# Message passing over 200,000 edges: nodes of layer 0 normalised once, 5 and 3 of 68 tiles fetched by column copies, edge features loaded three blocks at a time

## The reference

```python
edge_index = jnp.stack([src, dst])
h = relu(layernorm(x))
# layer 0
agg = segment_sum(h[src], dst)
x = x + agg @ W_rel.T + b_rel + h @ W_root.T
h = relu(layernorm(x))
# layer 1
edge_weights = silu(edge_attr_50 @ We1 + be1) @ We2 + be2
agg = segment_sum(h[src] * edge_weights, dst)
x = x + (h + silu(agg @ Wn1 + bn1) @ Wn2 + bn2)
```

## Time and profile before

| | |
|---|---|
| median of 3 runs | 5615.37 us (5615.32 to 5629.94) |
| span of the profiled execution, first to last instruction | 3996.3 us |
| that execution's own time with what lies around the span | not given by the profile |
| gathers | 2 x 1564, 67% of the chain that ended last |
| layer 0, first to last gather | 3.5 to 1964.1 us |
| layer 1, first to last gather | 2011.3 to 3976.7 us |
| busy: POOL, PE, DVE, ACT | 2976, 2447, 1995, 1187 us |

### The profile page before, as it was taken

How to read it: one execution, slowest core, us unless ns; L and a number is a source line. 1 busy time by engine, 2 the same in 40 slices (tenths; PEclk the granted TensorE clock), 3 DMA queues, 4 the chain that set the end, 5 groups by cost and what they waited for, 6 DMA issues and landing times.

```text
span 3996.3 us, 52113 instructions
## 1 busy us (share of the span) xinstructions
PE 2447.1 (61%) x10946; PEld 1882.0 (47%) x10946; DVE 1995.0 (50%) x6931; ACT 1187.2 (30%) x2730; POOL 2976.2 (74%) x3135
## 2 busy tenths in 40 slices
PE   3444444444444444444467788877887777887787
PEld 2334333333433333433445555555555555555555
DVE  6555555555555555555554444444444444444444
ACT  3444444444444444444411111111111111111111
POOL 7777777777777777777567777777777777777776
PEclk8555555555555555555578788788788887888878
DMA  2222222222222222222122222222222222222222
GB/s 84 62 61 61 61 64 67 61 61 61 61 64 67 61 61 61 61 66 64 50 78 78 83 80 79 81 76 83 78 80 82 77 75 83 80 79 82 77 76 82
DMA packets 208083, 284.73 MB, mean 71 GB/s; under 512 B 70338, under 2 KB 137972, under 8 KB 207828
## 3 DMA queue, kind: packets, MB, share of 16 engines
q0 software_dynamic: 100096, 205.20, 18.1%
q1 hardware_dynamic: 66676, 58.00, 4.9%
q10 hardware_dynamic: 41184, 20.45, 1.7%
HBM read 262.97 MB, written 20.45 MB: 71 GB/s over the span
## 4 chain that ended last, share of the span: by engine, by line
POOL 67%; issue 23%; PE 5%; DMA 2%; DVE 1%; POOLq 1%; ACT 0%; SPq 0%; DVEq 0%; ACTq 0%
POOL rows L298 67%; PE hid_ps L368 2%; PE seg_a L330 1%; PE ew_ps L373 1%; DMA rows<-h_rows,idx 1%; PE seg_b L330 1%; DMA ef<-ef_blocks 1%; POOLq L176 1%; POOLq L177 0%; DVE rows L670 0%; DVE onehot L566 0%; DVE ew_ps L666 0%; ACT hidden L502 0%; PE node_t L382 0%; ACT rows L436 0%
## 5 line engine op out<-in xcount | busy, mean ns | idle before, releaser
L298 POOL DMA_INDIRECT rows<-h_rows,idx x1564 | 1490.0, 953 | 522.6 <-issue 515.6
L298 POOL DMA_INDIRECT rows<-x,idx x1564 | 1485.2, 950 | 478.2 <-issue 478.2
L330 PE MATMUL seg_a<-onehot,rows 128*128 128x128 f32 x3312 | 726.6, 388 | 915.0 <-DVE onehot L566 408.1
L330 PEld LDWEIGHTS seg_a<-onehot,rows 128*128 128x128 f32 x3312 | 623.7, 281 | 1148.5 <-issue 960.0
L330 PE MATMUL seg_b<-onehot,rows 128*128 128x128 f32 x2944 | 606.4, 370 | 530.9 <-DVE onehot L566 374.4
L424 ACT ACTIVATE rows<-rows,e_shift,e_rstd 128x128 f32<-128x128 f32 x1564 | 643.3, 481 | 793.0 <-DVE e_shift L593 793.0
L330 PEld LDWEIGHTS seg_b<-onehot,rows 128*128 128x128 f32 x2944 | 520.8, 266 | 727.6 <-issue 448.3
L502 ACT ACTIVATE hidden<-hid_ps,be_col 128x512 f32<-128x512 f32 x391 | 268.8, 687 | 1416.1 <-PE hid_ps L368 1415.8
L373 PE MATMUL ew_ps<-we_sb,hidden 128*128 128x128 f32 x3128 | 539.8, 330 | 49.1 <-ACT hidden L502 49.1
L582 DVE BATCH_NORM_STATS2 e_stats<-rows 128x6 f32<-128x128 f32 x1564 | 339.7, 280 | 426.1 <-DMA rows<-x,idx 361.8
L368 PE MATMUL hid_ps<-ef,we_sb 50*128 50x512 f32 x782 | 522.7, 753 | 39.4 <-DMA ef<-ef_blocks 39.4
(11 more groups left out here) (91 smaller groups left out, 811.5 us busy)
## 6 DMA issues: line engine op xcount, KB each, us to landing
ef<-ef_blocks SPq DMA_DIRECT2D x391, 100.0 KB
rows<-x,idx POOLq DMA_INDIRECT x1564, 2.5
rows<-h_rows,idx POOLq DMA_INDIRECT x1564, 2.5
xs<-x SPq DMA_DIRECT2D x26, 256.0 KB
y_rows<-ys ACTq DMA_DIRECT2D x26, 256.0 KB, 2.5
ys<-y_rows SPq DMA_DIRECT2D x26, 256.0 KB, 3.3
out<-xs ACTq DMA_DIRECT2D x26, 256.0 KB
h_rows<-h1s ACTq DMA_DIRECT2D x24, 256.0 KB, 2.5
```

The costliest lines, as they stand in the source:

```text
L298: pool.indirect_dma_start(out=rows[:, u, t, :], out_offset=None, in_=table, in_offset=bass.IndirectOffsetOnAxis(ap=idx[:, j:j + 1], axis=0 ...
L330: mm = pe.matmul(seg[u % 2][:, 0:P], rows[:, u, t, :], onehot[:, u % 2, t, :], start=(t == 0), stop=(t == TB - 1))
```

## The change

Three parts.

- **Layer 0 is normalised per node.** A new phase ahead of layer 0 takes the 25 node groups of `x` through statistics, shift and ReLU once (five sets of buffers, `H_SETS`), stores them to a new table `h_rows` in HBM, turns them on PE and copies the turned groups into `agg[1]`, which is free during layer 0 (`h_table`: one column to a node). Iteration 0 of layer 0 works as before on rows of `x`; iterations 1 to 22 gather from `h_rows` and have no edge statistics and no ReLU. `node_update0` takes its turned group from `h_table`.
- **Some tiles are not gathered.** In iterations 1 to 22 of layer 0 the last 5 of the 68 tiles, in layer 1 the last 3, are made from the table in SBUF: an engine reads 16 node numbers from `cp_idx` into registers and copies 16 single columns (128 x 1) of the table into `act_cols` or `dve_cols`, eight times for a tile. ACT makes 3 tiles in layer 0 and 2 in layer 1, DVE 2 and 1. PE turns a finished tile into PSUM, and ACT copies it from there into `rows` (`rows_turned`). For layer 1 the table (`agg[0]`) is filled between the layers by 25 groups of turns of `h1_rows`.
- **Edge features** come in loads of three blocks into two buffers, in place of one block into four slots.

```diff
-EF_SLOTS = 4
+EF_BLOCKS = 3
+EF_GROUPS = -(-U // EF_BLOCKS)
+H_SETS = 5
+CHUNK = 16
+CHUNKS = P // CHUNK
+H_BY_ACT = (3, 4)
+CP_ACT = (3, 2)
+CP_DVE = (2, 1)
+CP_TILES = CP_ACT[0] + CP_DVE[0]
+CP_FIRST = U * TB - CP_TILES
...
+        cp_idx = sb("cp_idx", [ITERS, CP_TILES * P], I32)
+        act_cols, dve_cols = sb("act_cols", [P, 3 * P]), sb("dve_cols", [P, 2 * P])
...
+        ef = [sb("ef_a", [D_EDGE, EF_BLOCKS, BLOCK])[:, :, :], node_work[0:D_EDGE, :, :]]
...
+        h_table, h1_table = agg[1], agg[0]
...
+        def indices(engine, it, first, count):
+
+            row = bass.at_runtime_partition(cp_idx[0:1, first:first + count], it)
+            _, values = nc.values_load_multi_w_load_instructions(
+                row, engines=[engine], min_val=0, max_val=N_NODES - 1,
+                skip_runtime_bounds_check_because="edge sources are node numbers")
+            return values
...
@@ SP, ahead of layer 0
+            def load_h(k, r):
+                sp.dma_start(h_x[r], node_group(x, k * H_SETS + r)).then_inc(s_hx[r], 16)
+
+            def store_h(k, r):
+                hold(sp, s_hh, k * H_SETS + (r + 1))
+                sp.dma_start(node_group(h_rows, k * H_SETS + r), h_out[r]).then_inc(s_hstore[r], 16)
...
@@ SP, layer 1
-                        hold(sp, s_hid, slot_free(i, u, EF_SLOTS))
-                        sp.dma_start(ef[:, u % EF_SLOTS, :],
-                                     ef_blocks[bass.ds(it * U + u, 1)].rearrange("k c e -> c (k e)")
-                                     ).then_inc(s_ef[u % EF_SLOTS], 16)
+                        g, blocks = u // EF_BLOCKS, min(EF_BLOCKS, U - u)
+                        if u % EF_BLOCKS == 0:
+                            hold(sp, s_hid, done(i, u - EF_BLOCKS - 1) if g else done(i, EF_BLOCKS * (EF_GROUPS - 1) - 1 - U))
+                            sp.dma_start(ef[g % 2][:, 0:blocks, :],
+                                         ef_blocks[bass.ds(it * U + u, blocks)].rearrange("k c e -> c k e")
+                                         ).then_inc(s_ef[g % 2], 16)
...
@@ POOL
             with pool.Fori(0, passes_so_far) as p:
-                with pool.Fori(0, ITERS) as it:
-                    gather(0, x, p * ITERS + it, 0)
+                gather(0, x, p * ITERS, p * ITERS, U * TB, first=True)
+                for r in range(H_SETS):
+                    hold(pool, s_hstore[r], 16 * (GROUPS // H_SETS + 1))
+                with pool.Fori(1, ITERS) as it:
+                    i = p * ITERS + it
+                    gather(0, h_rows, i, i, CP_FIRST)
...
-                    gather(1, h1_rows, p * ITERS + it, passes * ITERS)
+                    i = p * ITERS + it
+                    gather(1, h1_rows, i, passes * ITERS + i, U * TB - CP_ACT[1] - CP_DVE[1])
...
@@ PE
+            with pe.Fori(0, GROUPS // H_SETS) as k:
+                for r in range(H_SETS):
+                    n = k * H_SETS + r
+                    pe.wait_ge(s_tcopy[r], k + 1)
+                    pe.wait_ge(s_tx[r], k * 16 + 16)
+                    for t in range(TB):
+                        tr = pe.transpose(h_turn[r][:, t * P:(t + 1) * P], t_rows[r][:, t, :], ident[:, :])
+                    tr.then_inc(s_tturn, 1)
...
@@ ACT
+            def columns(layer, table, n, it, c):
+                k, q = c // CHUNKS, c % CHUNKS
+                if q == 0:
+                    act.wait_ge(s_act_turn[layer], n * CP_ACT[layer] + (k + 1))
+                tile = (0, CP_TILES - CP_ACT[1] - CP_DVE[1])[layer] + k
+                for e, v in enumerate(indices(mybir.EngineType.Activation, it, tile * P + q * CHUNK, CHUNK)):
+                    at = k * P + q * CHUNK + e
+                    op = nc.scalar.activation(act_cols[:, at:at + 1], table[:, bass.ds(v, 1)], ACT.Copy)
+                if q == CHUNKS - 1:
+                    op.then_inc(s_cp_act[layer], 1)
+
+            def columns_at(layer, u):
+                total, last = CP_ACT[layer] * CHUNKS, U - 2
+                return [c for c in range(total) if c * last // total == u]
...
-                    edge_std(i, 0)
                     for u in range(U):
                         if u in steps:
                             steps[u]()
-                        edge_relu(i, u)
-                        if u + 1 < U:
-                            edge_std(i, u + 1)
+                        for c in columns_at(0, u):
+                            columns(0, h_table, n, it, c)
+                    rows_turned(0, n, i)
...
@@ DVE, layer 0, iterations 1 to 22
                     for u in range(U):
                         one_hot(0, i, it, u)
-                        if u + 2 < U:
-                            edge_stats(i, u + 2)
-                        if u + 1 < U:
-                            edge_shift(i, u + 1)
+                        for c in columns_at(0, u):
+                            columns(0, h_table, cp_count(0, p, it), it, c)
                         add_window(0, i, it, u)
...
@@ DVE, layer 1
                     for u in range(U):
                         one_hot(1, i, it, u)
+                        for c in columns_at(1, u):
+                            columns(1, h1_table, i, it, c)
                         message(i, u)
                         add_window(1, i, it, u)
```

More of the change, by code:

```diff
@@ L467, in _ @@
+            with act.Fori(0, passes) as p:
+                i = p * ITERS
+                steps = node_update0(loop_group(0), i, 0, done(i, TURN_AT - 1), i + 1)
+                edge_std(p * U, 0)
+                for u in range(U):
+                    if u in steps:
+                        steps[u]()
+                    edge_relu(p * U, u)
+                    if u + 1 < U:
+                        edge_std(p * U, u + 1)
+                with act.Fori(1, ITERS) as it:
                     i = p * ITERS + it
+                    n = cp_count(0, p, it)
@@ L480, in _ @@
                               for r, g in enumerate(late_groups(j))])
+            with act.Fori(0, GROUPS // H_SETS) as k:
+                for r in H_BY_ACT:
+                    act.wait_ge(s_tturn, k * H_SETS + (r + 1))
+                    nc.scalar.activation(h1_table[:, bass.ds(k * (H_SETS * BLOCK) + r * BLOCK, BLOCK)],
+                                         h_turn[r][:, :], ACT.Copy).then_inc(s_tcopy[r], 1)
+            for r in range(H_SETS):
+                hold(act, s_tcopy[r], GROUPS // H_SETS + 1)
             def node_update1(g, n, r, issued):
@@ L634, in _, with columns_at @@
+            def columns_at(layer, u):
+                total, last = CP_DVE[layer] * CHUNKS, U - 2
+                return [c for c in range(total) if c * last // total == u]
             window_targets().then_inc(s_setup, 1)
             dve.wait_ge(s_setup, 9)
+            hold(dve, s_hh, GROUPS)
+            for r in range(H_SETS):
+                hold(dve, s_hcopy[r], GROUPS // H_SETS + 1)
+            dve.wait_ge(s_cp_idx, 16)
             with dve.Fori(0, passes) as p:
-                with dve.Fori(0, ITERS) as it:
+                i = p * ITERS
+                steps = node_update0(i, 0, i + 1)
+                edge_stats(p, 0)
+                edge_stats(p, 1)
+                edge_shift(p, 0)
+                for u in range(U):
+                    one_hot(0, i, 0, u)
+                    if u + 2 < U:
+                        edge_stats(p, u + 2)
+                    if u + 1 < U:
+                        edge_shift(p, u + 1)
+                    add_window(0, i, 0, u)
+                    if u in steps:
+                        steps[u]()
+                with dve.Fori(1, ITERS) as it:
@@ L661, in _ @@
             dve.wait_ge(s_setup, 10)
+            with dve.Fori(0, GROUPS // H_SETS) as k:
+                for r in range(H_SETS):
+                    if r not in H_BY_ACT:
+                        dve.wait_ge(s_tturn, k * H_SETS + (r + 1))
+                        v.tensor_copy(h1_table[:, bass.ds(k * (H_SETS * BLOCK) + r * BLOCK, BLOCK)],
+                                      h_turn[r][:, :]).then_inc(s_tcopy[r], 1)
+            for r in range(H_SETS):
+                hold(dve, s_tcopy[r], GROUPS // H_SETS + 1)
             def message(i, u):
@@ L716 @@
     src_cols = src_pad.reshape(-1, P).T
+    cp_src = src_pad.reshape(ITERS, -1)[:, CP_FIRST * P:]
     arrays = {
```

379 lines of the change are left out of this document (285 added, 94 removed).

## The result

The changed kernel takes 6402.07 us (median of 3 runs, 6400.97 to 6404.87), the kernel before 5615.37: a ratio of 1.139, 95% interval 1.137 to 1.141. It is slower, where 5445 us and "faster" were forecast. One thing has to be known to read the numbers. In each session here, on one chip, all kernels ran in one of two conditions: in one the kernel before takes 3994 to 4001 us, in the other 5615 to 5669; I call them free and held up. One chip was met in both, and within a session the runs of one kernel agree to 0.8%. The times of both kernels above come from held-up sessions, the profile of the kernel before from a free one. That is the whole of the 1619 us that the prediction carried over: in a free session of its own the kernel before has a median of 4001.18 beside a span of 3998.8.

The account below looks back on a forecast made before the run. POOL's gathers, 1.25 us apart, were taken to pace both layers. First layer 1 message at 1917, plus 22.96 x 82.4, plus 16, gave span 3825, 171 less; 5615.4 - 171 = 5445 us, range 5285 to 5690.

Parts of the forecast that it names:

- The gathers: POOL, both layers: gathers start 1.25 us apart, 63 and 65 an iteration; removing some saves 224 us if nothing else binds.
- the sign of being wrong: POOL: waiting for segment sums through a whole layer would show the forecast wrong; waits were expected only around iteration 1.
- I carry the difference over unchanged: Whole kernel: the 1619 us between profiled span 3996.3 and median 5615.4 stay as they are after the change.
- the rest belongs to the gathers: Rival, POOL: the 1619 us are longer gathers, 1.77 us each, so 316 us go, time 5295; chance 0.24.
- Price of a column copy: DVE and ACT: 0.10 us for each one-column copy, a chunk of 16 with its load 2.1 us, bounds 2.0 to 3.9.
- Load of 16 numbers: Register load from cp_idx on DVE and ACT: 0.5 us for a load and its drain.
- a load costs by the number: Rival, cp_idx loads: 0.305 us for each number, 4.9 us a load, time 8130 us; chance 0.09.
- So POOL stays the bound: Layer 0: DVE's 70.7 us and ACT's 59 stay under POOL's 78.75 an iteration, so the copies cost nothing.
- 3.6 + chunk: Layer 1, DVE: 17 blocks of 3.6 us plus 8 chunks, 16.8 us, and small parts make 82.4 us an iteration.
- the second rival: Layer 1: chunk ahead of the message, PE at lower clock; 98.5 us an iteration, time 5814 us, slower; chance 0.16.
- Start, layer change, sum: First segment sum at 93 us, hidden; first layer 1 message at 1917; span 3825, 171 us less than 3996.
- The edge features: Both layers: loading edge features three blocks at a time changes neither layer's sum; nothing.

Follow-up runs that it names:

- f3: Changed kernel with two tiles on ScalarE, two on VectorE in layer 0, and one on VectorE alone in layer 1: 4459.57 us free, ratio 1.115.
- f1: Changed kernel without VectorE's tiles in layer 0, and VectorE's layer 1 chunk moved behind the message: 4069.39 us free, ratio 1.018.
- f2: Changed kernel with one VectorE tile fewer in each layer (3+1 and 2+0): 3827.17 us free, ratio 0.957; 6005.00 held up, 1.059.
- session 5: Held up; changed kernel with only ScalarE's three layer 0 tiles, in short hardware loops: 6424.13 us, ratio 1.133, layer 1 132.2 us an iteration.
- the padded one: Kernel before plus 30 copies of a constant column on ScalarE behind each block's activation in layer 1: 5735.59 us held up, ratio 1.020.
- act0: Changed kernel with only ScalarE's three tiles in layer 0, no other column copies, written out: 3912.03 us free, ratio 0.978.

## Why the prediction was wrong

**The gathers: right.** 1.25 us apart, 63 and 65 an iteration. That POOL waits for segment sums through a whole layer was the sign of being wrong, and it does, in both layers when held up and in layer 1 when free.

**"I carry the difference over unchanged": wrong.** The 1619 us lie inside the layers: an iteration of layer 0 takes 102.5 us held up against 85.0, and one of layer 1 some 137.6 against 85.1; 23 of each make 1610 us. They are not a rest that stays when the kernel changes: the changed kernel takes 1910 us more held up than free. Nor does "the rest belongs to the gathers" hold: a gather is as long, and by the packet records its last packet ends 2.2 us after its start in either condition. What is longer are waits for signals and, in places, the distances of instructions beside a burst. The timeline of POOL and of ScalarE in the changed kernel:

```profile
1452.39 0.95 POOL L384 DMA_INDIRECT rows<-h_rows,idx  x1 [2.78 <-PE seg_b L441]
...
1467.48 0.95 POOL L384 DMA_INDIRECT rows<-h_rows,idx  x1 [0.30 <-issue]
1474.18 0.94 POOL L384 DMA_INDIRECT rows<-h_rows,idx  x1 [5.75 <-PE seg_a L441]
```

```profile
1453.02 1.67 ACT L655 ACTIVATE act_cols<-agg 128x1 f32 x16 [1.01 <-issue]
...
1462.98 0.20 ACT L655 ACTIVATE act_cols<-agg 128x1 f32 x1 [0.52 <-issue]
...
1468.10 0.20 ACT L655 ACTIVATE act_cols<-agg 128x1 f32 x1 [0.54 <-issue]
1468.79 0.20 ACT L655 ACTIVATE act_cols<-agg 128x1 f32 x1 [0.49 <-issue]
1470.65 1.67 ACT L655 ACTIVATE act_cols<-agg 128x1 f32 x16 [1.65 <-issue]
```

The gathers run from 1452.4 to 1468.4 but for one pause of 1.64. The copies are undisturbed for the first 5 us, then they crawl, and the chunk from 1470.65 on runs through again. A kernel that adds 42 thousand instructions beside the gathers pays for that: in layer 0 98.9 us an iteration without copies, 117.3 with three tiles on ScalarE and one on VectorE, 118.4 with two on VectorE.

**Price of a column copy: nearly right. Load of 16 numbers: put at half of what it is.** The sequencers' loads and the copies in the free session:

```profile
L223 ACTq TENSOR_LOAD <-cp_idx x896: 1005/1030/1612, 157.8 to 4460.2; - x180
L223 DVEq TENSOR_LOAD <-cp_idx x536: 1094/1121/1511, 163.4 to 4458.6; - x179
L913 DVE COPY dve_cols<-agg x8576: 152/154/157, 164.6 to 4461.9; 128x1 f32 x200
L668 ACTq FUSED_REGOPS x14336: 37/37/43, 158.8 to 4462.8; - x200
```

In chunks that run through, 16 copies take 1.87 us on DVE and 1.67 on ACT, of which the last is 0.15 and 0.19: 0.114 and 0.099 apart, 0.10 forecast. The load takes 1.12 on DVE and 1.03 on ACT, where "0.5 for a load and its drain" stood. DVE hides half of it beside a one-hot (0.61 idle), ACT nothing. A chunk is 2.48 and 2.70 us, 2.1 forecast, in the range of 2.0 to 3.9. The rival that a load costs by the number was right in kind: (1.12 - 0.305) / 15 = 0.054 us for each number more, against 0.305 by that rival. The Trainium skill, page "Runtime: NRT & Kernel Launch", section "Instruction fetch mechanics", has about 200 ns a register even in bulk. That would be 3.2 us for 16, an estimate by that page; the trace has a third of it, so the trace decides.

**Layer 0: the sign was right, the size not.** "So POOL stays the bound" with 59 us on ACT and 70.7 on DVE. By the measured chunk ACT has 24 x 2.70 + 9 = 74, DVE 16 x 2.48 + 37 = 77, and their waits for each other come on top: 83.9. One tile less on either engine, and it is the pace of the gathers or nearly so: 80.0 with 3+1, 81.2 with 2+2 (64 gathers, 80.0). Three on ScalarE alone hide under 65 gathers. Five tiles are one too many. What failed is the reading that an engine whose own sum lies under 78.75 costs nothing: both measured sums do, and the iteration takes 83.9. Which of the waits between them ends last in the full kernel stays open. That one tile less on VectorE gives 80.0 and one less on ScalarE still 81.2, 1.2 over its gathers, says that neither engine alone is the bound.

**Layer 1: the step that failed.** It is "3.6 + chunk": a block of 3.57 us where rows have landed, and a chunk on top, 82.4 us an iteration in all. It takes 104.6 free and 151.3 held up. The dearer chunk (2.48 for 2.1) is 3 of the 22 us; the rest is a block that does not stay at 3.6. The timeline of DVE and PE in the free session:

```profile
3289.12 1.15 PE L448 MATMUL seg_a<-onehot,rows 128*128 128x128 f32 x8 [0.39 <-DVE rows L983]
3290.11 1.06 PE L536 MATMUL ew_ps<-we_sb,hidden 128*128 128x128 f32 x8
3290.62 0.68 DVE L848 TENSOR_TENSOR onehot<-iota_ps,dst_rel 128x512 f32<-128x512 f32 x1
3291.91 1.87 DVE L913 COPY dve_cols<-agg 128x1 f32 x16 [0.61 <-issue]
3293.73 0.70 DVE L975 TENSOR_TENSOR ew_ps<-ew_ps,be_all 128x512 f32<-128x512 f32 x1
3294.47 0.69 DVE L983 TENSOR_TENSOR rows<-ew_ps,rows 128x512 f32<-128x512 f32 x1
3295.29 2.07 PE L448 MATMUL seg_b<-onehot,rows 128*128 128x128 f32 x8 [3.07 <-DVE rows L983]
3297.16 1.91 PE L536 MATMUL ew_ps<-we_sb,hidden 128*128 128x128 f32 x8
3297.50 0.29 DVE L859 TENSOR_TENSOR agg<-seg_b,agg 128x128 f32 x1 [2.34 <-PE seg_b L448]
3297.71 0.68 DVE L848 TENSOR_TENSOR onehot<-iota_ps,dst_rel 128x512 f32<-128x512 f32 x1
3299.11 0.70 DVE L975 TENSOR_TENSOR ew_ps<-ew_ps,be_all 128x512 f32<-128x512 f32 x1 [0.72 <-PE ew_ps L536]
3299.84 0.69 DVE L983 TENSOR_TENSOR rows<-ew_ps,rows 128x512 f32<-128x512 f32 x1
```

PE's segment sum and weights take 1.15 and 1.06 us in the first two lines, the upper of its two levels, 2.4 GHz. Then PE waits 3.07 us for the message that stands behind the chunk, and its next segment sum and weights take 2.07 and 1.91, the lower level, 1.2 GHz. DVE waits for each of them, so even the block without a chunk, 3294.47 to 3299.84, takes 5.37 us and not 3.6; the 161 blocks that take 6 to 9 us, most of them with a chunk, have a median of 7.45 where 5.7 was forecast. The lower level is met more often with the chunk, but not only with it: over 18 iterations of layer 1, 183 of the 306 segment sums of the changed kernel take more than 1.6 us, 198 of those of f3, 121 of f1, 73 of f2 and 90 of the kernel before. Where VectorE has no chunk, the rows have landed and the clock is at its upper level, the chain has its 3.6 us again, as in f2:

```profile
3003.64 0.69 DVE L981 TENSOR_TENSOR rows<-ew_ps,rows 128x512 f32<-128x512 f32 x1
3005.68 0.29 DVE L857 TENSOR_TENSOR agg<-seg_b,agg 128x128 f32 x1 [1.35 <-PE seg_b L448]
3005.89 0.68 DVE L846 TENSOR_TENSOR onehot<-iota_ps,dst_rel 128x512 f32<-128x512 f32 x1
3006.48 0.69 DVE L973 TENSOR_TENSOR ew_ps<-ew_ps,be_all 128x512 f32<-128x512 f32 x1
3007.21 0.69 DVE L981 TENSOR_TENSOR rows<-ew_ps,rows 128x512 f32<-128x512 f32 x1
```

This was the second rival, with its place (the chunk ahead of the message), its cause (PE's clock) and its point of decision, 90.6 us; it had 98.5 us an iteration, and 104.6 are measured. It stood at 0.16: the forecast took over a block at the clock of layer 1 before, 0.80, for a layer with other idle times. Its mechanism was right and its time, 5814 us, was not: it too had layer 0 at 78.75 us an iteration and carried the 1619 us over, and the end that it put at 4195 us of the span came at 4491. f1 puts the chunk beside the segment sum and has 90.8; even there eight chunks cost 8.5 us against f2. ScalarE's 16 chunks cost layer 1 nothing that f2 shows (82.3 for 66 gathers, 82.5).

**Start, layer change, sum.** The first segment sum is at 101.2 us, 93 forecast. The first message comes at 2076.7, where 1917 were forecast. The last gather of layer 0 starts 99 us later than forecast (1925.5 for 1826.6), and the last window add, at 2007.4, lies 82 us behind it and not 12.5 as before; the way from there to the first message is 8 us shorter than forecast. From the first to the last message are 2401 us (1951 in the earlier trace rows, 1892 forecast). In sum 4491.0 - 3996.3 = 495 us are lost: 48 by the first message, 450 in layer 1, and 2 gained back behind the last message. Held up, the 787 us between the two medians are some 407 by the first gather of layer 1 (2860 for 2453) and some 380 behind it. Two sums of the prediction are a few us off, which changes nothing: 5615.4 - 171 is 5444, and the scaled gathers give 5299.

**The edge features: right when free, wrong when held up.** Nothing in free sessions (85.1 and 85.2). Held up, layer 1 without copies differs in its loop by these loads alone and takes 131.4 us against some 137.6, which is an estimate; 132.2 in session 5. The sum had "nothing".

## What to carry to other kernels

Work added to an engine under the bound is only free if it does not stand between two steps of a serial chain through PE: there it costs its own length, and where PE's clock falls the blocks beside it are longer too (5.4 us for 3.6 here). Put such work on the engine whose next step has slack (ScalarE's two tiles), behind the step that feeds PE, and count the chain at the lower clock before calling it covered. And when the timed runs and the profiled execution differ by more than a per cent, get one run in which they agree before building on either.

## What the runs showed of the hardware

- The held-up condition. While gathers run back to back, instructions of ScalarE, VectorE and SP stand 0.70 us or 1.40 us apart in places, from some 5 us after the start of a burst until some time after its end (0.4 us in the stretch of the changed kernel above, 5.8 in that of the padded one); the kernel before loses 40%. In the changed kernel's held-up trace the instructions that the queues work themselves (register operations, loads, DMA issues) start 0.68 to 0.73 us after the one before 745 times on ScalarE, 682 on VectorE and 242 on SP; in its free trace 8, 52 and 3 times. It hits constant copies and short loops that fetch no block too. It does not hit all: of VectorE's copies 426 of 5632 stand so in layer 0 and 1 of 2944 in layer 1, of ScalarE's 587 of 8448 and 268 of 5888. It holds up signals too: in the padded kernel's layer 0, which is the kernel before, a BN_AGGR waits 3.20 us for the statistics of its own engine, which the earlier trace rows show without a wait:

```profile
1228.79 0.86 DVE L585 BATCH_NORM_STATS2 e_stats<-rows 128x6 f32<-128x128 f32 x4
...
1232.85 0.38 DVE L589 BATCH_NORM_AGGREGATE e_mv<-e_stats 128x2 f32<-128x6 f32 x4 [3.20 <-remote]
```

  What makes a session held up stays open: nothing in the kernel does, since one chip showed both. The traces of such sessions also hold fewer records of semaphores (20.5 thousand updates for the changed kernel, against 59.1 thousand in a free session), so many waits end by "remote" or by an unknown queue, and the recording itself can't be excluded as the cause; every time here is taken with it.
- A register load of 16 numbers takes 1.03 to 1.12 us, of one number 0.305; a copy of one column 0.099 us on ScalarE and 0.114 on VectorE from start to start.
- Fetching a long body anew in each iteration stays hidden behind the gathers in a free session: act0, with some 850 instructions an iteration on ScalarE in layer 0 and 211 instruction blocks fetched in the run, keeps to the pace of the gathers. What it would cost on an engine that is the bound no run here shows.
